# A selective-scan stage on one core: two 512-column scans per step become one of 1024 columns

## The chip, the core and the metric

The program runs on one core of one Trainium2 chip. The metric is the device time of one execution in microseconds (us). Engines: TensorE (PE), VectorE (DVE), ScalarE (ACT), GpSimd (POOL), and SyncE (SP), which here only issues DMAs.

## The reference

The program has two layers. The change lies in the first half of layer 1, a Mamba-like block over 4096 tokens in four sequences of 1024, with 512 channels and 16 states per channel. In short (x, z, B, C and dt come from projections of the normalised input):

```python
x     = silu(conv4(in_proj(h)))
dt    = softplus(wd2(wd1(x)) + bias)
decay = exp(dt * A)                 # per token, channel, state; A = -exp(A_log)
h[t]  = decay[t] * h[t-1] + dt[t] * x[t] * B[t]
y[t]  = sum over states (h[t] * C[t]) + W_D * x[t]
out   = out_w(y * silu(skip))
```

The recurrence starts from zero at the beginning of each sequence. Layer 0 (a gated recurrent block and an MLP) comes before it, a mixture of eight experts after it.

## The kernel before

Function `mamba` holds channels on the 128 partitions (so 512 channels are KE = 4 tiles) and tokens on the free axis. Tokens are cut into NCH = 8 chunks of T = 512; chunks 2k and 2k+1 are the two halves of sequence k. A chunk q has NU = 32 steps n, one for each state (NST = 16) and each pair of channel tiles (HALF = 2); u = 32q + n counts the steps. Of step u:

- POOL (`inputs`, L1103): `bx[u % 5] = ux * B`, 128x1024, that is two tiles of 512 columns. It works up to NB = 5 steps ahead, bound by `s_scan`.
- ACT (`decay`, L1251): two exponentials of 512 columns, one for each tile, into one of NA = 4 PSUM tiles `da`. The tile is free when the scan that used it two steps earlier is done.
- DVE (L1387): two scans of 512 columns, `hh = da * previous + bx`. In even chunks they start from 0.0, in odd chunks from `carry`, the last column of the same state in the chunk before, which ACT saved (`keep`, L1260).
- PE (`spread`, L1460): C[t] to all partitions, into the single PSUM tile `cb`.
- DVE (L1395): `hc = hh * cb`, 128x1024.
- PE (L1486): adds `hc` into `y` by a product with the identity.

After steps 16 and 32 of a chunk DVE forms `y * silu(skip)` (`finish`, L1373).

The order of the work is written out by hand, and each engine takes its own instructions in that order. Besides the steps, each engine has work for other chunks at fixed step numbers (`extra` on ACT and POOL, `pieces` on PE). Those that matter here:

- ACT, n = 0 to 11: convolution taps of chunk q+1 (`taps`, L1150, L1152), skip tiles (`take_skip`, L1159), n = 10 and 12: two output tiles of chunk q-1 (`take_out`, L1197), n = 12: `silu` (a table load, L1164, L1165, a table load back at the next exponential), n = 25: the exponential and logarithm of the softplus (L1226, a table load, L1229).
- POOL, n = 1, 4, 7, 10: sums of the taps (`conv`, L1032, L1034), which wait for ACT's taps; n = 26: L1083, which waits for ACT's L1229; n = 24 to 31: further softplus work (L1077, L1088, L1050) and, every five steps, an indirect DMA (L1112).
- PE: a projection piece on even n. One PSUM tile `rb` serves them all, so a piece waits until ACT has copied the one before.

ACT runs two steps ahead with its exponentials. Its loop is:

```python
for u in range(STEPS):
    if u + 2 < STEPS:
        decay(u + 2, 0)
    keep(u)
    if u + 2 < STEPS:
        decay(u + 2, 1)
    extra(u // NU, u % NU)
```

Of the kernel before, what the change touches and what calls it, by code (L numbers as in the profile page):

```python
# [6 lines left out]
P = 128  # L7
F32 = mybir.dt.float32
# [4 lines left out]
ALU = mybir.AluOpType  # L13
ACT = mybir.ActivationFunctionType
# [6 lines left out]
T = 512  # L21
NCH = NTOK // T
# [712 lines left out]
NST = 16  # L735
# [13 lines left out]
def mamba(nc, dram):  # L749
# [5 lines left out]
    HALF = KE // 2  # L755
    NB = 5
    NA = 4
    NG = 4
    NU = 2 * NST
# [16 lines left out]
    turn = {key: k for k, key in enumerate(order)}  # L776
# [3 lines left out]
    with ExitStack() as ctx:  # L780
        def sb(name, shape, dt=F32):
            return ctx.enter_context(nc.sbuf_tensor("m_" + name, shape, dt))

        def sem(name):
            return ctx.enter_context(nc.semaphore("m_" + name))

        y = ctx.enter_context(nc.psum_tensor("m_y", [P, HALF, T], F32))
        da = [ctx.enter_context(nc.psum_tensor(f"m_da{i}", [P, T], F32)) for i in range(NA)]
        cb = ctx.enter_context(nc.psum_tensor("m_cb", [P, T], F32))
        rb = ctx.enter_context(nc.psum_tensor("m_rb", [P, T], F32))  # L790
        dram["held"] = ExitStack()
# [11 lines left out]
        A = sb("A", [P, KE * NST])  # L803
# [12 lines left out]
        dl = [sb(f"dl{h}", [P, KE, T]) for h in range(2)]  # L816
# [9 lines left out]
        bx, hc = work[:, 0:NB], work[:, NB:NB + 4]  # L826
        rows = sb("rows", [P, 2, REC])
        hh = sb("hh", [P, 2, HALF, T])
        mo = sb("mo", [P, 2, D])
        mo2 = hh[:, 0, 0].rearrange("p (s d) -> p s d", d=D)  # L830
        dst = sb("dst", [P, NPICK], I32)
        carry = sb("carry", [P, NST, KE])

        plan = hc.rearrange("p a b t -> p (a b t)")
        used = [0]

        def part(shape, dt=F32):
# [6 lines left out]
            if dt is not F32:  # L844
# [21 lines left out]
        filled, drained = sem("filled"), sem("drained")  # L866
# [4 lines left out]
                                                         sem("s_hc"), sem("s_y"))  # L871
        s_y1, s_diag, s_hi, s_res, s_mid, s_low = (sem("s_y1"), sem("s_diag"), sem("s_hi"), sem("s_res"), sem("s_mid"),
                                                   sem("s_low"))
        block = ctx.enter_context(nc.Block())

        def wait_filled(eng, g, p):
# [131 lines left out]
        def _(pool):  # L1008
# [83 lines left out]
            def inputs(u):  # L1092
                q, n = u // NU, u % NU
                if n % NST == 0:
                    pool.wait_ge(s_ux, 2 * q + n // NST + 1)
                if n % NG == 0:
                    G = u // NG
                    pool.wait_ge(b_in[G % 2], 16 * (G // 2 + 1))
                if u >= NB:
                    pool.wait_ge(s_scan, (u - NB + 1) * HALF)  # L1100
                cols = slice(HALF * (n // NST), HALF * (n // NST + 1))
                slot = bb[:, (u // NG) % 2, n % NG:n % NG + 1]
                pool.tensor_tensor(bx[:, u % NB], ux[q % 2][:, cols], slot.to_broadcast([P, HALF, T]), ALU.mult).then_inc(s_bx, 1)  # L1103
# [26 lines left out]
        def _(act):  # L1130
# [109 lines left out]

            def decay(u, i):
                q, n = u // NU, u % NU
                if n % NST == 0 and i == 0:
                    act.wait_ge(s_dl, 2 * q + n // NST + 1)
                    act.wait_ge(s_A, 1)
                d = u * HALF + i
                if d >= NA:
                    act.wait_ge(s_scan, d - NA + 1)
                e = HALF * (n // NST) + i
                at = e * NST + n % NST  # L1250
                act.activation(da[d % NA][:], dl[q % 2][:, e], ACT.Exp, scale=A[:, at:at + 1]).then_inc(s_exp, 1)  # L1251

            def keep(u):
                q, n = u // NU, u % NU
                if q % 2 == 0:
                    act.wait_ge(s_scan, (u + 1) * HALF)
                    if q >= 2:
                        act.wait_ge(s_scan, (u - NU + 1) * HALF)
                    j = n // NST
                    act.activation(carry[:, n % NST, HALF * j:HALF * (j + 1)], hh[:, u % 2, :, T - 1], ACT.Copy).then_inc(s_carry, 1)  # L1260

            act.wait_ge(s_pad, 1)
            for q, n in slots[:8 + NU]:
                if (q, n) == (-1, 27):
                    extra(q, n)
                    for u in range(2):
                        decay(u, 0)
                        decay(u, 1)
                    continue
                extra(q, n)  # L1270
                if (q, n) == (-2, 28):
                    act.wait_ge(s_d, 2 * NJ + 1)
                    act.activation(ex[:, 1], ex[:, 0], ACT.Exp).then_inc(s_ex, 1)
# [6 lines left out]
                extra(u // NU, u % NU)  # L1280
            take_out(NCH - 1, 0)
            wait_filled(act, "O1", NCH - 1)
            act.activation(mo2, da[0][:].rearrange("p (s d) -> p s d", s=2), ACT.Copy).then_inc(drained, 1)

        @block.vector
        def _(dve):
# [9 lines left out]
            def over(row, k):  # L1296

                return row.rearrange("p (o n) -> p o n", o=1).to_broadcast([row.shape[0], k, row.shape[1]])

            dve.wait_ge(lg_in, 16)  # L1300
            for j in range(NJ):
                step(dve.max(m8[:, j], lg[:, j]), False)
# [72 lines left out]
            for u in range(STEPS):  # L1375
                q, n = u // NU, u % NU
                j = n // NST
                dve.wait_ge(s_bx, u + 1)
                if u >= 2:
                    dve.wait_ge(s_hc, u - 1)  # L1380
                if u >= 2 and ((u - 2) // NU) % 2 == 0:
                    dve.wait_ge(s_carry, (u - 2) // NU // 2 * NU + (u - 2) % NU + 1)
                for i in range(HALF):
                    d = u * HALF + i
                    e = HALF * j + i
                    dve.wait_ge(s_exp, d + 1)
                    dve.tensor_tensor_scan(hh[:, u % 2, i], da[d % NA][:], bx[:, u % NB, i],  # L1387
                                           0.0 if q % 2 == 0 else carry[:, n % NST, e:e + 1], ALU.mult, ALU.add).then_inc(s_scan, 1)
                dve.wait_ge(s_cb, u + 1)
                dve.wait_ge(s_scan, (u + 1) * HALF)  # L1390
                if u >= 4:
                    dve.wait_ge(s_y, u - 3)
                else:
                    dve.wait_ge(s_out, 32)
                dve.tensor_tensor(hc[:, u % 4], hh[:, u % 2],  # L1395
                                  cb[:].rearrange("p (o t) -> p o t", o=1).to_broadcast([P, HALF, T]), ALU.mult).then_inc(s_hc, 1)
                if n == 0 and q > 0:
                    finish(q - 1, 1)
                if n == NST:
                    finish(q, 0)  # L1400
# [3 lines left out]
        def _(pe):  # L1404
# [5 lines left out]
            pe.wait_ge(s_diag, KE)  # L1410

            def piece(g, p):
                to = da[0] if (g, p) == ("O1", NCH - 1) else rb
                if turn[g, p] > 0 and to is rb:
                    pe.wait_ge(drained, turn[g, p])
                if g[:2] in ("IN", "SK"):
                    e = int(g[2:])
                    if g == "IN0":
                        pe.wait_ge(xr_in, p * 16 + 16)
                    col = (E_IN if g[:2] == "IN" else 0) + e * P  # L1420
                    for k in range(KD):
                        last = mm(rb[:], w_si[:, k, col:col + P], xr[:, k], start=(k == 0), stop=(k == KD - 1))
                elif g == "BD":
                    if p == 0:
                        pe.wait_ge(w_in, 16 * len(w_loads))
                    pe.wait_ge(s_silu, 2 * p + 1)
                    for e in range(KE):
                        last = mm(rb[0:DR + 2 * NST, :], w_x[:, e], xs[p % 2][:, e], start=(e == 0), stop=(e == KE - 1))
                elif g[:2] == "DT":
                    e = int(g[2:])  # L1430
                    wait_drained(pe, "BD", p)
                    last = mm(rb[:], w_dt[:, e * P:(e + 1) * P], dr, start=True, stop=True)
                else:
                    j = int(g[1:])
                    pe.wait_ge(s_y1, 2 * p + 2)
                    pe.wait_ge(res_in, 16 * (p + 1))
                    for s in (2 * j, 2 * j + 1):
                        at = slice((s % 2) * D, (s % 2 + 1) * D)
                        mm(to[:, at], ident[:], xres[:, s], start=(s % 2 == 0), stop=False, skip_group_check=True)
                        for e in range(KE):  # L1440
                            last = mm(to[:, at], y1[e // HALF][p % 2][:, e % HALF, s * P:(s + 1) * P], w_out[:, e],
                                      start=False, stop=(e == KE - 1 and s % 2 == 1), skip_group_check=True)
                last.then_inc(filled, 1)
# [28 lines left out]
            for u in range(STEPS):  # L1472
                q, n = u // NU, u % NU
                j = n // NST
# [441 lines left out]
```

## Time and profile before

| | us |
|---|---|
| median of three executions | 2537.9 (2536.19 to 2542.38) |
| profiled execution, its own span | 2537.0 |
| first scan of the step loop starts | 819.0 |
| last scan of the step loop starts | 1806.9 |
| PE, DVE, ACT, POOL busy over the span | 2135.7, 1956.4, 1376.4, 1328.8 |

The profile's span covers the first to the last instruction, and the profiled execution agrees with the median within 1 us. "Busy" is time in which an engine executed; the share over the whole span mixes the stages, so the step loop is read by itself. In a row of the timeline the numbers are the start, the time to the end of the group, engine, line, operation, written and read tensors; "x2" says that two instructions stand in one row, and a bracket gives the idle time before it and who ended it.

### The profile page before, as it was taken

What the parts mean: (1) busy time and instruction counts of PE and PEld (TensorE: products, weight loads), DVE (VectorE), ACT (ScalarE), POOL (GpSimd) and SP (SyncE); (2) the same over time, 40 slices, a digit from 0 to 9 for tenths busy, and PEclk for the clock granted to TensorE, in tenths of its full rate; (3) what the DMA queues carried; (4) which work ended last, traced back from release to release, by engine and by line L of the source; (5) the groups of instructions that cost most, each with busy time, mean ns of one, the idle gap of its engine ahead of it and who ended that gap; (6) DMA issues with size and microseconds to landing.
All of it is one profiled execution on the core that took longest, in us unless ns stands there. A gap on an engine that the chain in (4) does not pass through costs nothing. (4 is left out here: it accounts for less than half of the span.)

```text
span 2537.0 us, 35012 instructions
## 1 busy us (share of the span) xinstructions
PE 2135.7 (84%) x10706; PEld 1539.2 (61%) x10706; DVE 1956.4 (77%) x2684; ACT 1376.4 (54%) x2333; POOL 1328.8 (52%) x953
## 2 busy tenths in 40 slices
PE   2699999999975788788878887867599999999995
PEld 1578777787751334333334333323399999999995
DVE  6644565545645999989898999899688888888883
ACT  1322233222326676667666666653277777777672
POOL 1112221122206999898989899997213333334433
PEclk8899999999987999999999999999899999999998
DMA  8010111101122213232223232314166667667663
GB/s 267 17 42 0 41 41 41 41 0 41 41 68 89 105 69 109 75 105 77 100 77 103 75 105 75 115 57 165 59 240 227 206 228 235 208 222 236 212 216 88
DMA packets 108971, 286.66 MB, mean 113 GB/s; under 512 B 20550, under 2 KB 85462, under 8 KB 90022
## 3 DMA queue, kind: packets, MB, share of 16 engines
q1 hardware_dynamic: 94598, 267.12, 30.1%
q0 software_dynamic: 14304, 18.75, 3.6%
q8 instruction: 27, 0.44, 0.1%
q14 instruction: 42, 0.34, 0.0%
HBM read 239.21 MB, written 50.82 MB: 114 GB/s over the span
## 5 line engine op out<-in xcount | busy, mean ns | idle before, releaser
L1103 POOL TENSOR_TENSOR m_work<-m_ux,m_bb 128x1024 f32<-128x1024 f32 x256 | 598.5, 2358 | 24.7 <-DVE m_hh L1387 22.1
L1251 ACT ACTIVATE m_da<-m_dl,m_A 128x512 f32<-128x512 f32 x512 | 349.3, 687 | 279.6 <-DVE m_hh L1387 278.8
L1486 PE MATMUL m_y<-m_work,m_ident 128*128 128x512 f32 x1024 | 493.0, 604 | 1.5 <-DVE m_work L1395 1.5
L1806 PE MATMUL e_h<-e_xTh,e_w1h 128*128 128x256 f32 x1248 | 353.4, 283 | 7.2 <-DVE e_xTl L1742 6.5
L1395 DVE TENSOR_TENSOR m_work<-m_hh,m_cb 128x1024 f32<-128x1024 f32 x256 | 312.7, 1222 | 48.8 <-PE m_cb L1460 25.6
L1806 PE MATMUL e_h<-e_xTl,e_w1h 128*128 128x256 f32 x1248 | 349.4, 280 | 0.0
L1806 PE MATMUL e_h<-e_xTh,e_w1l 128*128 128x256 f32 x1248 | 349.3, 280 | 0.0
L1387 DVE TENSOR_TENSOR_SCAN m_hh<-m_da,m_carry,m_work 128x512 f32<-128x512 f32 x256 | 313.9, 1268 | 7.4 <-POOL m_work L1103 7.3
L1387 DVE TENSOR_TENSOR_SCAN m_hh<-m_da,m_work 128x512 f32<-128x512 f32 x256 | 298.3, 1208 | 13.4 <-POOL m_work L1103 13.4
L1486 PEld LDWEIGHTS m_y<-m_work,m_ident 128*128 128x128 f32 x1024 | 198.3, 194 | 161.0 <-issue 147.9
L281 POOL TENSOR_TENSOR small<-mv,eps_ln 128x4 f32<-128x4 f32 x17 | 3.4, 201 | 551.3 <-DVE mv L399 551.3
L1460 PE MATMUL m_cb<-m_bc,m_sel 96*128 96x512 bf16 x256 | 98.3, 384 | 192.5 <-DVE m_work L1395 192.1
L1702 ACT ACTIVATE e_sg<-e_h,e_b 128x256 f32<-128x256 f32 x312 | 146.4, 470 | 187.1 <-PE e_h L1806 187.1
L1806 PEld LDWEIGHTS e_h<-e_xTh,e_w1h 128*128 128x128 f32 x1248 | 237.4, 190 | 8.0 <-DVE e_xTl L1742 5.3
L1460 PEld LDWEIGHTS m_cb<-m_bc,m_sel 96*128 96x128 bf16 x256 | 24.7, 96 | 356.8 <-DVE m_work L1395 343.0
L1806 PEld LDWEIGHTS e_h<-e_xTl,e_w1h 128*128 128x128 f32 x1248 | 235.6, 189 | 0.0
L1806 PEld LDWEIGHTS e_h<-e_xTh,e_w1l 128*128 128x128 f32 x1248 | 235.3, 189 | 0.0
L1759 DVE SCALAR_TENSOR_TENSOR e_ac<-e_h,e_b,e_sg 128x256 f32<-128x256 f32 x312 | 149.4, 479 | 44.6 <-ACT e_sg L1702 44.1
L1817 PE MATMUL e_o<-e_w2h,e_ach 128*128 128x256 f32 x624 | 174.1, 279 | 0.0
L1587 POOL DMA_INDIRECT scratch_mo<-e_yo,e_place x78 | 160.8, 2062 | 24.4 <-issue 11.9
L1817 PE MATMUL e_o<-e_w2h,e_acl 128*128 128x256 f32 x624 | 173.3, 278 | 0.0
L1817 PE MATMUL e_o<-e_w2l,e_ach 128*128 128x256 f32 x624 | 173.1, 277 | 0.0
(275 smaller groups left out, 4801.0 us busy)
## 6 DMA issues: line engine op xcount, KB each, us to landing
m_bb<-scratch_bT SPq DMA_DIRECT2D x64, 1024.0 KB
m_first<-in_w SPq DMA_DIRECT2D x20, 2048.0 KB, 7.5
e_w<-in_w SPq DMA_DIRECT2D x19, 2048.0 KB, 7.4
m_first<-in_w SPq DMA_DIRECT2D x20, 1024.0 KB, 10.1
e_w<-in_w SPq DMA_DIRECT2D x19, 1024.0 KB, 10.0
scratch_rec<-x1p SPq DMA_DIRECT2D x39, 260.0 KB, 8.3
e_xg<-scratch_rec SPq DMA_DIRECT2D x39, 260.0 KB, 2.8
e_b<-in_b SPq DMA_DIRECT2D x39, 128.0 KB, 3.0
```

What stands on the lines that cost most here:

```text
L281: pool.tensor_tensor(sm[:, 0], var, eps_ln[:], ALU.add).then_inc(done, 1)
L1103: pool.tensor_tensor(bx[:, u % NB], ux[q % 2][:, cols], slot.to_broadcast([P, HALF, T]), ALU.mult).then_inc(s_bx, 1)
L1251: act.activation(da[d % NA][:], dl[q % 2][:, e], ACT.Exp, scale=A[:, at:at + 1]).then_inc(s_exp, 1)
L1387: dve.tensor_tensor_scan(hh[:, u % 2, i], da[d % NA][:], bx[:, u % NB, i], 0.0 if q % 2 == 0 else carry[:, n % NST, e:e + 1], ALU.mult, AL ...
L1395: dve.tensor_tensor(hc[:, u % 4], hh[:, u % 2], cb[:].rearrange("p (o t) -> p o t", o=1).to_broadcast([P, HALF, T]), ALU.mult).then_inc(s_ ...
L1460: mm(cb[:], sel[:, at:at + 1].to_broadcast([3 * 2 * NST, P]), bc3[q % 2][:], start=True, stop=True).then_inc(s_cb, 1)
L1486: last = mm(y[:, i], ident[:], hc[:, u % 4, i], start=False, stop=(n % NST == NST - 1))
L1587: pool.indirect_dma_start(dram["mo"][:, :], bass.IndirectOffsetOnAxis(ap=place[i][:, s:s + 1], axis=0), yo[i][:, s, :], None, compute_op=A ...
L1702: act.activation(sg[:, m % 2], hbank[m % HR][:, 1], ACT.Silu, bias=b1[i][:, KF + m:KF + m + 1]).then_inc(s_sg, 1)
L1759: dve.scalar_tensor_tensor(out=ac[:, m % 2], in0=hbank[m % HR][:, 0], scalar=b1[i][:, m:m + 1], in1=sg[:, m % 2], op0=ALU.add, op1=ALU.mul ...
L1806: last = mm(hbank[m % HR][:, j], w[i][:, k, cols], x[i][:, k], start=(p == 0 and k == 0 and j == 0), stop=(p == 2 and k == KD - 1 and j == 1),
L1817: last = mm(obank[i][:, s], a[i][:, m, s * P:(s + 1) * P], w[i][:, m], start=(m + s + p == 0), stop=(p == 2 and m == KF - 1 and s == NS - ...
```

## The change

The four `da` tiles become one PSUM tensor of 4 x 512 columns, so that the pair of a step is 1024 adjacent columns. DVE makes one scan over both tiles of a step. So that the second tile doesn't continue from the end of the first, its first decay column is zero: it is written once, at the start, and the exponential of tile 1 writes columns 1 to 511 only. In odd chunks tile 1 has a carry of its own; ACT adds `a0 * carry` to the first column of its `bx` (one 128x1 instruction per step, `a0` being 16 first decays, computed in one 128x16 exponential for each half of an odd chunk). This new instruction stands on ACT ahead of the exponential of tile 1 and waits for POOL's `bx` of its step. Both exponentials of a step now wait for the one scan two steps earlier.

```diff
-        da = [ctx.enter_context(nc.psum_tensor(f"m_da{i}", [P, T], F32)) for i in range(NA)]
+        da = ctx.enter_context(nc.psum_tensor("m_da", [P, NA, T], F32))
...
+        a0 = sb("a0", [P, HALF, NST])
...
                 if u >= NB:
-                    pool.wait_ge(s_scan, (u - NB + 1) * HALF)
+                    pool.wait_ge(s_scan, u - NB + 1)
...
             def decay(u, i):
                 q, n = u // NU, u % NU
+                j = n // NST
+                e = HALF * j + i
                 if n % NST == 0 and i == 0:
-                    act.wait_ge(s_dl, 2 * q + n // NST + 1)
+                    act.wait_ge(s_dl, 2 * q + j + 1)
                     act.wait_ge(s_A, 1)
+                    if q % 2 == 1:
+                        act.activation(a0[:, j], A[:, (e + 1) * NST:(e + 2) * NST], ACT.Exp,
+                                       scale=dl[q % 2][:, e + 1, 0:1]).then_inc(s_a0, 1)
                 d = u * HALF + i
-                if d >= NA:
-                    act.wait_ge(s_scan, d - NA + 1)
-                e = HALF * (n // NST) + i
+                if u >= 2:
+                    act.wait_ge(s_scan, u - 1)
+                if q % 2 == 1 and i == 1:
+                    act.wait_ge(s_bx, u + 1)
+                    act.wait_ge(s_a0, q // 2 * 2 + j + 1)
+                    act.wait_ge(s_carry, q // 2 * NU + n + 1)
+                    head = bx[:, u % NB, 1, 0:1]
+                    act.activation(head, carry[:, n % NST, e:e + 1], ACT.Identity, scale=a0[:, j, n % NST:n % NST + 1],
+                                   bias=head).then_inc(s_fix, 1)
                 at = e * NST + n % NST
-                act.activation(da[d % NA][:], dl[q % 2][:, e], ACT.Exp, scale=A[:, at:at + 1]).then_inc(s_exp, 1)
+                act.activation(da[:, d % NA, i:T], dl[q % 2][:, e, i:T], ACT.Exp, scale=A[:, at:at + 1]).then_inc(s_exp, 1)
...
-                for i in range(HALF):
-                    d = u * HALF + i
-                    e = HALF * j + i
-                    dve.wait_ge(s_exp, d + 1)
-                    dve.tensor_tensor_scan(hh[:, u % 2, i], da[d % NA][:], bx[:, u % NB, i],
-                                           0.0 if q % 2 == 0 else carry[:, n % NST, e:e + 1], ALU.mult, ALU.add).then_inc(s_scan, 1)
+                dve.wait_ge(s_exp, (u + 1) * HALF)
+                if u == 0:
+                    dve.wait_ge(s_cut, HALF)
+                if q % 2 == 1:
+                    dve.wait_ge(s_fix, q // 2 * NU + n + 1)
+                pair = slice(u % 2 * HALF, u % 2 * HALF + HALF)
+                e = HALF * j
+                dve.tensor_tensor_scan(hh[:, u % 2].rearrange("p e t -> p (e t)"), da[:, pair].rearrange("p e t -> p (e t)"),
+                                       bx[:, u % NB].rearrange("p e t -> p (e t)"),
+                                       0.0 if q % 2 == 0 else carry[:, n % NST, e:e + 1], ALU.mult, ALU.add).then_inc(s_scan, 1)
```

ACT's instructions around step 12 of an odd chunk, before; L1251 is an exponential of `decay`, L1197 `take_out`, L1164 and L1165 `silu`:

```order
L1197 ACTIVATE m_mo<-m_rb 128x512 [waits m_filled]
L1251 ACTIVATE m_da<-m_dl,m_A 128x512 [waits m_s_scan] x4
L1197 ACTIVATE m_mo<-m_rb 128x512 [waits m_mo_out,m_filled]
L1164 ACT_TABLE_LOAD [waits m_drained]
L1164 ACTIVATE m_xs<-m_spare 128x2048 [waits m_s_cv]
L1165 ACTIVATE m_sk<-m_sk 128x2048
L1251 ACT_TABLE_LOAD
L1251 ACTIVATE m_da<-m_dl,m_A 128x512 [waits m_s_scan] x2
```

The same place of the changed program (lines have moved: L1264 is the exponential, L1261 the new 128x1 instruction, L1199 `take_out`, L1166 and L1167 `silu`):

```order
L1199 ACTIVATE m_mo<-m_rb 128x512 [waits m_filled]
L1264 ACTIVATE m_da<-m_dl,m_A 128x512 [waits m_s_scan]
L1261 ACTIVATE m_work<-m_carry,m_work,m_a 128x1 [waits m_s_a0,m_s_carry,m_s_bx,m_s_scan]
L1264 ACTIVATE m_da<-m_dl,m_A 128x511
L1264 ACTIVATE m_da<-m_dl,m_A 128x512 [waits m_s_scan]
L1261 ACTIVATE m_work<-m_carry,m_work,m_a 128x1 [waits m_s_a0,m_s_carry,m_s_bx,m_s_scan]
L1264 ACTIVATE m_da<-m_dl,m_A 128x511
L1199 ACTIVATE m_mo<-m_rb 128x512 [waits m_mo_out,m_filled]
L1166 ACT_TABLE_LOAD [waits m_drained]
L1166 ACTIVATE m_xs<-m_spare 128x2048 [waits m_s_cv]
L1167 ACTIVATE m_sk<-m_sk 128x2048
L1264 ACT_TABLE_LOAD
```

What moved: between any two extras of an odd chunk there now stands an instruction that waits for `s_bx`, POOL's product.

DVE around step 0 of an odd chunk, before:

```order
L1387 SCALAR_TENSOR_TENSOR m_hh<-m_da,m_carry,m_work 128x512 [waits m_s_carry,m_s_exp,m_s_hc,m_s_bx]
L1387 SCALAR_TENSOR_TENSOR m_hh<-m_da,m_carry,m_work 128x512 [waits m_s_exp]
L1395 TENSOR_TENSOR m_work<-m_hh,m_cb 128x1024 [waits m_s_y,m_s_scan,m_s_cb]
L1373 TENSOR_TENSOR m_y<-m_y,m_sk 128x1024 [waits m_s_silu,m_s_y]
L1387 SCALAR_TENSOR_TENSOR m_hh<-m_da,m_carry,m_work 128x512 [waits m_s_carry,m_s_exp,m_s_hc,m_s_bx]
```

And after, the scan (L1406) of two steps:

```order
L1406 SCALAR_TENSOR_TENSOR m_hh<-m_da,m_carry,m_work 128x1024 [waits m_s_exp,m_s_carry,m_s_fix,m_s_hc,m_s_bx]
```

What moved: one instruction of 1024 columns stands where two of 512 stood, and it waits for both exponentials and for the new instruction (`s_fix`).

## Rows read from the trace of the kernel before

**Rows 1.** The page, part 1: busy us (share of the span) xinstructions.

```profile
PE 2135.7 (84%) x10706; PEld 1539.2 (61%) x10706; DVE 1956.4 (77%) x2684; ACT 1376.4 (54%) x2333; POOL 1328.8 (52%) x953
```

**Rows 2.** Stretches, chunks 1 and 7: length, busy of PE, PEld, DVE, ACT, POOL, PE clock.

```profile
937.00:1062.30 125.30, 102.36 (x258) 44.56 (x256) 117.66 (x100) 82.82 (x116) 117.33 (x57) 0.97 0.26 90
...
1687.90:1811.00 123.10, 83.53 (x212) 36.50 (x212) 117.19 (x99) 42.70 (x62) 84.25 (x40) 0.97 0.27 98
```

**Rows 3.** Waits in the step loop: engine line waited for, us in total, times, longest.

```profile
DVE m_work L1395 <- PE m_cb L1460: 25.6, 18, 2.7
...
POOL m_spare L1083 <- ACT m_spare L1229: 21.1, 7, 3.7
DVE m_hh L1387 <- POOL m_work L1103: 20.7, 14, 4.5
```

**Rows 4.** Tile view of m_work: durations min/median/max in ns, first and last start, form.

```profile
L1387 DVE TENSOR_TENSOR_SCAN m_hh<-m_da,m_work x256: 1196/1207/1225, 819.0 to 1685.4; 128x512 f32<-128x512 f32 x128
...
L1387 DVE TENSOR_TENSOR_SCAN m_hh<-m_da,m_carry,m_work x256: 1257/1267/1284, 937.0 to 1806.9; 128x512 f32<-128x512 f32 x128
...
L1331 DVE TENSOR_TENSOR_SCAN m_work<-m_work x8: 260/270/2382, 760.9 to 764.4; 128x64 f32<-128x64 f32 x8
```

**Rows 5.** Timeline, DVE: a step of chunk 3, then one of chunk 4.

```profile
1291.85 2.45 DVE L1387 TENSOR_TENSOR_SCAN m_hh<-m_da,m_carry,m_work 128x512 f32<-128x512 f32 x2
1294.39 1.22 DVE L1395 TENSOR_TENSOR m_work<-m_hh,m_cb 128x1024 f32<-128x1024 f32 x1
...
1318.98 2.33 DVE L1387 TENSOR_TENSOR_SCAN m_hh<-m_da,m_work 128x512 f32<-128x512 f32 x2
...
1321.40 1.22 DVE L1395 TENSOR_TENSOR m_work<-m_hh,m_cb 128x1024 f32<-128x1024 f32 x1
```

**Rows 6.** Groups by line and form, ACT: count, busy us, mean ns, idle before.

```profile
L1150 ACT ACTIVATE m_spare<-m_first,m_vec 128x512 f32<-128x512 f32 x84 | 57.0, 711 | 31.7 <-issue 31.7
...
L1260 ACT ACTIVATE m_carry<-m_hh 128x2 f32<-128x2 f32 x128 | 26.0, 203 | 37.8 <-DVE m_hh L1387 37.6
...
L1152 ACT ACTIVATE m_spare<-m_first,m_vec 128x512 f32<-128x512 f32 x28 | 22.5, 803 | 0.0
```

**Rows 7.** Timeline of chunk 1, steps 10 to 15: POOL, then ACT, then DVE.

```profile
992.09 4.69 POOL L1103 TENSOR_TENSOR m_work<-m_ux,m_bb 128x1024 f32<-128x1024 f32 x2
...
989.45 0.58 ACT L1197 ACTIVATE m_mo<-m_rb 128x512 f32<-128x512 f32 x1
990.05 1.28 ACT L1164 ACT_TABLE_LOAD   x1
992.16 1.91 ACT L1164 ACTIVATE m_xs<-m_spare 128x2048 f32<-128x2048 f32 x1 [0.83 <-POOL m_spare L1034]
993.98 1.90 ACT L1165 ACTIVATE m_sk<-m_sk 128x2048 f32<-128x2048 f32 x1
995.89 1.28 ACT L1251 ACT_TABLE_LOAD   x1
997.19 3.15 ACT L1251 ACTIVATE m_da<-m_dl,m_A 128x512 f32<-128x512 f32 x5
...
998.17 1.28 DVE L1387 TENSOR_TENSOR_SCAN m_hh<-m_da,m_carry,m_work 128x512 f32<-128x512 f32 x1
```

**Rows 8.** Timeline: POOL's product and DVE's scan, chunk 3, then chunk 5.

```profile
1240.88 2.36 POOL L1103 TENSOR_TENSOR m_work<-m_ux,m_bb 128x1024 f32<-128x1024 f32 x1
...
1249.85 1.28 DVE L1387 TENSOR_TENSOR_SCAN m_hh<-m_da,m_carry,m_work 128x512 f32<-128x512 f32 x1
...
1492.44 4.67 POOL L1103 TENSOR_TENSOR m_work<-m_ux,m_bb 128x1024 f32<-128x1024 f32 x2
...
1499.62 1.28 DVE L1387 TENSOR_TENSOR_SCAN m_hh<-m_da,m_carry,m_work 128x512 f32<-128x512 f32 x1
```

**Rows 9.** Timeline of chunk 1, step 25: ACT, then POOL.

```profile
1039.61 1.04 ACT L1226 ACTIVATE m_spare<-m_spare 128x1024 f32<-128x1024 f32 x1
...
1044.02 2.35 POOL L1083 TENSOR_TENSOR m_spare<-m_spare 128x1024 f32<-128x1024 f32 x1 [2.45 <-ACT m_spare L1229]
```

More of the change, by code:

```diff
@@ L873, in mamba @@
                                                    sem("s_low"))
+        s_cut, s_a0, s_fix = sem("s_cut"), sem("s_a0"), sem("s_fix")
         block = ctx.enter_context(nc.Block())
@@ L1255, in keep @@
                 if q % 2 == 0:
-                    act.wait_ge(s_scan, (u + 1) * HALF)
+                    act.wait_ge(s_scan, u + 1)
                     if q >= 2:
-                        act.wait_ge(s_scan, (u - NU + 1) * HALF)
+                        act.wait_ge(s_scan, u - NU + 1)
                     j = n // NST
@@ L1262, in _ @@
             act.wait_ge(s_pad, 1)
+            act.wait_ge(s_cut, HALF)
             for q, n in slots[:8 + NU]:
@@ L1282, in _ @@
             wait_filled(act, "O1", NCH - 1)
-            act.activation(mo2, da[0][:].rearrange("p (s d) -> p s d", s=2), ACT.Copy).then_inc(drained, 1)
+            act.activation(mo2, da[:, 0].rearrange("p (s d) -> p s d", s=2), ACT.Copy).then_inc(drained, 1)
         @block.vector
@@ L1298, in over @@
                 return row.rearrange("p (o n) -> p o n", o=1).to_broadcast([row.shape[0], k, row.shape[1]])
+            for i in range(HALF):
+                dve.memset(da[:, 2 * i + 1, 0:1], 0.0).then_inc(s_cut, 1)
             dve.wait_ge(lg_in, 16)
@@ L1382, in _ @@
                     dve.wait_ge(s_carry, (u - 2) // NU // 2 * NU + (u - 2) % NU + 1)
-                for i in range(HALF):
-                    d = u * HALF + i
-                    e = HALF * j + i
-                    dve.wait_ge(s_exp, d + 1)
-                    dve.tensor_tensor_scan(hh[:, u % 2, i], da[d % NA][:], bx[:, u % NB, i],
-                                           0.0 if q % 2 == 0 else carry[:, n % NST, e:e + 1], ALU.mult, ALU.add).then_inc(s_scan, 1)
+                dve.wait_ge(s_exp, (u + 1) * HALF)
[8 more added lines that the diff above has]
+                                       0.0 if q % 2 == 0 else carry[:, n % NST, e:e + 1], ALU.mult, ALU.add).then_inc(s_scan, 1)
                 dve.wait_ge(s_cb, u + 1)
-                dve.wait_ge(s_scan, (u + 1) * HALF)
+                dve.wait_ge(s_scan, u + 1)
                 if u >= 4:
@@ L1412, in piece @@
             def piece(g, p):
-                to = da[0] if (g, p) == ("O1", NCH - 1) else rb
-                if turn[g, p] > 0 and to is rb:
+                own = (g, p) == ("O1", NCH - 1)
+                to = da[:, 0] if own else rb[:]
+                if turn[g, p] > 0 and not own:
                     pe.wait_ge(drained, turn[g, p])
```

## The prediction

> **What bounds the kernel now.** I read the page first [rows 1]: over the span PE is the busiest engine, but that is a mean over stages, and the change touches only the step loop. So I cut the loop into its eight chunks. In chunk 1 DVE is busy 117.66 and POOL 117.33 of 125.30 us; in chunk 7, where POOL has no work for a next chunk, POOL needs only 84.25 while DVE needs 117.19 of 123.10 [rows 2]. Two engines are nearly full, so the waits decide. DVE waits 20.7 us for POOL's products and 25.6 us for the spread C; POOL in turn waits 21.1 us, 3 us in each of seven chunks, for ACT's logarithm [rows 3]. The chain of a chunk is therefore a ring, not one engine: ACT's work of step 25, which begins with L1226 at 1039.61 and goes through a table load and L1229, releases POOL's L1083 at 1044.02 after 2.45 us of idleness [rows 9]; POOL then runs without a pause through its softplus and convolution work up to the steps near 14 of the next chunk, where DVE has caught up with it; from there DVE goes at its own pace to step 25. A faster scan helps on the last arc alone. Chunk 7 is DVE's from its third step on, chunk 0 in all its steps.
>
> **What a scan of 1024 columns saves.** A 64-column scan takes 270 ns and a 512-column one 1207: (1207 - 270) / 448 = 2.09 ns a column, 136 ns fixed. So 1024 columns are 2.28 us, and 60 ns more with a carry (1267 against 1207) [rows 4]. Two scans of 512 take 2.33 us together without and 2.45 with a carry, since the second begins before the first has ended; the product L1395 follows 0.09 us later in both [rows 5]. The saving is 2.33 - 2.28 = 0.05 us a step in even chunks and 2.45 - 2.34 = 0.11 in odd ones: 128 x 0.16 = 20.5 us if every step counted. The Trainium skill (VectorE: DVE Perf Modes, the section on the fixed extra latency per instruction) says that the latency is exposed between instructions and a large tile pays it once; with its fixed term of about 150 cycles, 156 ns, the saving would be 256 x 0.156 = 40 us. The trace shows most of the fixed time already overlapped.
>
> **What the change costs on ACT, even chunks.** Both exponentials of step u+2 now wait for the whole scan of step u. Before, the first ran during the second scan of the pair. So everything behind them on ACT comes one exponential later, 0.62 us (five take 3.15, the last 0.69: (3.15 - 0.69) / 4) [rows 7]. The step's own exponentials have slack: their scan comes a product, a scan and a product later, 1.22 + 2.3 + 1.22 = 4.7 us [rows 5]. What is late is the logarithm of step 25, and with it POOL's L1083 and the ring: +0.6 a chunk. Against it stand the DVE steps of the last arc, from about 17 to 25, 8 x 0.05 = 0.4. An even chunk comes out at +0.2; chunks 2, 4, 6: **+0.6**. Chunk 0 has 25 steps at DVE's pace, 1.25 - 0.6, with a little lost at the silu: **-0.5**.
>
> **The new instruction, odd chunks.** No 128x1 instruction with two per-partition operands is in the trace. A 128x2 copy takes 203 ns; a second such operand costs 803 - 711 = 92 ns [rows 6]. Bounds: 203 ns, and 203 + 2 x 92 = 387. I take 0.38, of which 0.1 overlaps the next: 0.28 on ACT's chain. The Trainium skill (ScalarE: Activation LUTs, what an ACTIVATE costs) gives 93 ns for each pointer operand, as the trace has it. The 32 steps of a chunk have 9 us of this on an engine that is idle a third of the time [rows 2], so the work itself is hidden.
>
> What isn't hidden is what it waits for. It waits for `bx` of step u+2 at ACT's step u, and `extra(u)` stands behind it. To cost nothing, `bx` would have to be ready when the exponential of tile 0 ends, 4.7 - 0.7 = 4 us before its scan. It isn't: the product of step 14 ends at 994.45, 1243.24 and 1494.8 in chunks 1, 3 and 5 [rows 7, 8], and the scan of step 14 starts one step of 3.68 (2.54 + 1.22, less the 0.08 by which a scan starts before the product ends) ahead of that of step 15: leads of 0.0, 2.9 and 1.1 us. So ACT's extras now follow POOL instead of DVE, and whoever waits for them is late: PE's pieces (rb is drained later), through them `cb`, and most of all the silu. In chunk 1 `bx` of step 14 is ready at 992.09 + half of 4.69, 994.45. Behind it on ACT: new instruction 0.28, exponential 0.62, take_out 0.60, table load 1.30, silu 1.82 and 1.91, table load 1.30 (starts 989.45, 990.05, 992.16, 993.98, 995.89, 997.19), exponential 0.62, new instruction 0.28, exponential 0.69, and 0.03 of signal: 9.45 us. The scan of step 15 can't start before 1003.9; before it started at 998.17 [rows 7]. That is +5.7. For chunk 3, 1243.24 + 9.45 against 1249.85: +2.8. For chunk 5, 1494.8 + 9.45 against 1499.62: +4.6 [rows 8]. DVE gets back 10 x 0.11 = 1.1 until the scan of step 25; the logarithm then comes 0.62 + 0.28 = 0.9 later behind it. Net -0.2 each: 5.5 + 2.6 + 4.4 = **+12.5**. POOL's own chain up to step 14 I leave as it is: the taps end about when the convolution asks for them.
>
> Chunk 7 has neither taps nor silu: 28 x 0.11 = **-3.1**.
>
> The rest costs nothing: two memsets at the start, two 128x16 exponentials for an odd chunk (about as long as the 203 ns copy, in idle ACT time), one scan semaphore in place of two.
>
> **Sum.** 12.5 + 0.6 - 0.5 - 3.1 = +9.5 us. The sum is made on the profiled execution (2537.0), 0.9 below the median; I put it on the median: 2547.4, and as POOL's chain can only suffer by late taps, **2548**.
>
> **Rivals.** *DVE sets the pace* (the other side). If POOL kept far enough ahead at steps 0 to 14 of the odd chunks, no wait of the new instruction would be seen, and the scan's saving would count in full: -20.5 us, 2517; half of it, 2528, if the ring keeps half. For it: DVE is at 94% in a chunk. Against it: 20.7 us of waiting for POOL, and a POOL as full as DVE. It decides from a lead of about 4 us. With the page's 156 ns it would be 2498. Chance 0.13.
>
> *The new wait is absorbed.* The silu's lateness finds slack that I don't see (DVE waits 25.6 us for PE, some of it just behind, at steps 10 to 12 and 16 [rows 3]). Then odd chunks lose 1 us or nothing: -3.1 - 0.5 + 0.6 + 3 = 0, so 2532 to 2541. Chance 0.27.
>
> *It goes round twice.* ACT's taps, too, stand behind `bx`, and POOL's convolution asks for them. From the `bx` of the step ahead of a tap pair ACT needs 0.28 + 0.62, two taps 1.2, 0.62 + 0.28 + 0.62 of the next step, and taps 0.62 + 0.80 plus a skip tile 0.6 at times: 5.0 to 5.6 us; POOL asks after two products, 4.7. At 0.3 to 0.9 us for each of four convolutions in three chunks that is 12 x 0.6 = 7 us on POOL's own arc, on top of my sum: 2555. Chance 0.15.
>
> My forecast, the silu behind `bx`, 2541 to 2553: 0.45.
>
> **Numbers.** A measurement of this kernel can tell about 0.3%, 7.6 us: faster is below 2530.3, slower above 2545.5. Faster 0.13 (first rival). Slower: 0.15 of the last rival and three quarters of my own, 0.34: 0.49. Same: 0.38. The range that leaves out 0.1 at either end is 2531 to 2559.
>
> **What the profile after would show.** Right: a scan of 1024 columns at 2.28 and 2.34 us; in odd chunks ACT's 128x1 instruction with idle time released by POOL's product; in chunks 1, 3, 5 a gap of several us before the scan of step 15, released by an exponential; POOL's L1083 later by the same; chunk 7 shorter by 3 us, odd chunks longer by 3 to 5.5, even ones unchanged. Wrong: if odd chunks have no gap before step 15, POOL was ahead and the silu was not the neck; if a 1024-column scan takes much more than 2.28 us, the linear price fell; if the even chunks change by over 1 us, the ring is read wrongly.

## The result and the profile after

The changed kernel takes 2553.82 us (median, 2553.12 to 2554.74), the kernel before 2538.26 in the same comparison: ratio 1.0059, 95% interval 1.0045 to 1.0073. It is slower by 15.6 us. 2548 was forecast, in a range of 2531 to 2559; the band that I gave to this cause alone, 2541 to 2553, is passed by 0.8 us.

The step loop, from the start of the first scan to the end of the last product L1395 (L1415 in the changed kernel), takes 1002.6 us in the profiled execution after and 990.5 before: +12.1. The whole span grew from 2537.0 to 2551.6. Of the 2.4 us that this leaves, 0.47 lie ahead of the loop and 1.95 behind it, in code that the change doesn't touch. That part behind it takes 727.5 us before, 729.5 after, and 728.1 to 729.6 in the twelve runs below; the profiled execution of before was a short one there. I therefore compare loops beside medians. A loop is that of one execution, though, and not only the edit moves it: chunks 0 and 4 of wait_at_14 below, in which nothing was edited, came out 1.2 and 1.1 us longer than before.

The groups of DVE's product and of its scans, from the profile page of the changed kernel (out<-in, count, busy us, mean ns, idle before):

```profile
L1415 DVE TENSOR_TENSOR m_work<-m_hh,m_cb 128x1024 f32<-128x1024 f32 x256 | 312.6, 1221 | 62.5 <-PE m_cb L1481 41.3
...
L1406 DVE TENSOR_TENSOR_SCAN m_hh<-m_da,m_carry,m_work 128x1024 f32<-128x1024 f32 x128 | 300.1, 2344 | 21.2 <-ACT m_da L1264 20.8
L1406 DVE TENSOR_TENSOR_SCAN m_hh<-m_da,m_work 128x1024 f32<-128x1024 f32 x128 | 292.3, 2283 | 18.3 <-POOL m_work L1105 16.5
```

The scan of 1024 columns takes 2.28 us and 2.34 with a carry, as the straight line through [rows 4] gave. DVE has less work, but before it never waited for ACT's exponentials and now it waits 20.8 us for them, and its wait for the spread C has grown from 25.6 [rows 3] to 41.3 us.

Stretches of the changed kernel, chunks 0 to 3 and 7 (columns as in [rows 2], where the last two are the share of the DMA engines and GB/s):

```profile
819.50:936.20 116.70, 88.70 (x208) 35.01 (x209) 110.82 (x66) 82.58 (x146) 108.02 (x53) 0.99 0.24 87
936.20:1068.90 132.70, 106.78 (x260) 45.80 (x259) 114.41 (x67) 90.47 (x151) 118.19 (x58) 0.95 0.24 85
1068.90:1192.60 123.70, 101.31 (x254) 44.20 (x254) 112.24 (x67) 83.26 (x149) 114.07 (x57) 0.97 0.27 93
1192.60:1324.80 132.20, 106.68 (x260) 45.68 (x259) 114.32 (x68) 90.44 (x151) 118.09 (x58) 0.95 0.24 85
...
1701.90:1824.00 122.10, 86.49 (x212) 37.52 (x212) 113.83 (x66) 49.83 (x95) 84.75 (x40) 0.94 0.27 99
```

Chunk 1 has gone from 125.3 to 132.7 us, its DVE work from 117.66 to 114.41. By the starts of their first scans the eight chunks changed by -1.3, **+7.4**, -0.6, **+4.5**, -0.1, **+4.6**, -1.1 and -1.3 us: the loss sits in chunks 1, 3 and 5 alone.

The place that was forecast, step 12 of chunk 1, timeline of ACT, then DVE, changed kernel:

```profile
994.75 0.39 ACT L1261 ACTIVATE m_work<-m_carry,m_work,m_a 128x1 f32<-128x1 f32 x1 [2.30 <-POOL m_work L1105]
995.04 0.67 ACT L1264 ACTIVATE m_da<-m_dl,m_A 128x511 f32<-128x511 f32 x1
995.65 0.57 ACT L1199 ACTIVATE m_mo<-m_rb 128x512 f32<-128x512 f32 x1
996.24 1.28 ACT L1166 ACT_TABLE_LOAD   x1
997.54 1.92 ACT L1166 ACTIVATE m_xs<-m_spare 128x2048 f32<-128x2048 f32 x1
999.36 1.89 ACT L1167 ACTIVATE m_sk<-m_sk 128x2048 f32<-128x2048 f32 x1
1001.27 1.28 ACT L1264 ACT_TABLE_LOAD   x1
1002.56 0.69 ACT L1264 ACTIVATE m_da<-m_dl,m_A 128x512 f32<-128x512 f32 x1
1003.19 0.37 ACT L1261 ACTIVATE m_work<-m_carry,m_work,m_a 128x1 f32<-128x1 f32 x1
1003.47 0.67 ACT L1264 ACTIVATE m_da<-m_dl,m_A 128x511 f32<-128x511 f32 x1
...
998.04 2.34 DVE L1406 TENSOR_TENSOR_SCAN m_hh<-m_da,m_carry,m_work 128x1024 f32<-128x1024 f32 x1
1000.47 1.22 DVE L1415 TENSOR_TENSOR m_work<-m_hh,m_cb 128x1024 f32<-128x1024 f32 x1
1004.34 2.35 DVE L1406 TENSOR_TENSOR_SCAN m_hh<-m_da,m_carry,m_work 128x1024 f32<-128x1024 f32 x1 [2.64 <-ACT m_da L1264]
```

ACT stands idle for 2.30 us until POOL's product, then the chain of [rows 7] follows link by link, and the scan of step 15 starts at 1004.34 instead of 998.17. Counted from the first scan of its chunk it comes 7.0, 4.2 and 6.1 us later in chunks 1, 3 and 5; that of step 14 comes 4.4, 2.2 and 4.1 us later. So a good part of the lateness is there ahead of the silu. The new instruction takes 0.37 to 0.39 us.

A second hole, at steps 4 to 6 of the same chunk; timeline of ACT, PE and DVE:

```profile
962.39 0.39 ACT L1261 ACTIVATE m_work<-m_carry,m_work,m_a 128x1 f32<-128x1 f32 x1 [1.82 <-issue]
...
964.61 0.57 ACT L1161 ACTIVATE m_sk<-m_rb 128x512 f32<-128x512 f32 x1
...
965.24 3.78 PE L1443 MATMUL m_rb<-m_xr,m_first 128*128 128x512 f32 x4 [6.02 <-ACT m_sk L1161]
968.81 0.64 PE L1481 MATMUL m_cb<-m_bc,m_sel 96*128 96x512 bf16 x1
...
969.49 1.22 DVE L1415 TENSOR_TENSOR m_work<-m_hh,m_cb 128x1024 f32<-128x1024 f32 x1 [3.58 <-PE m_cb L1481]
```

The skip tile (L1161) is copied late, since it too stands behind a wait for `bx`: the profile names no releaser for the 1.82 us ahead of L1261, but its start is 0.1 us behind the end of a product of POOL, 962.3. PE can't start its piece in `rb`, and DVE waits 3.58 us for the spread C behind the piece. The product that waits is that of step 6; the scan of step 7 comes late by it, hence "the hole at step 7" below. Chunks 3 and 5 have the same hole, with 3.48 and 3.40 us. I had named this path, but not priced it.

### The profile page after: what moved, and what is told of

The parts are those of the page before. It is cut to its first block and busy times, and to the rows that moved or that the text cites. A ratio compares the mean times of both kernels' runs of the same rounds, so it can differ in the third digit from the quotient of the medians.

```text
span 2551.6 us, 35270 instructions
## 1 busy us (share of the span) xinstructions
PE 2151.4 (84%) x10706; PEld 1543.8 (61%) x10706; DVE 1937.8 (76%) x2430; ACT 1396.6 (55%) x2469; POOL 1330.8 (52%) x953
## 5 line engine op out<-in xcount | busy, mean ns | idle before, releaser
L1264 ACT ACTIVATE m_da<-m_dl,m_A 128x512 f32<-128x512 f32 (+1 forms) x512 | 346.3, 679 | 245.3 <-DVE m_hh L1406 245.0
L1415 DVE TENSOR_TENSOR m_work<-m_hh,m_cb 128x1024 f32<-128x1024 f32 x256 | 312.6, 1221 | 62.5 <-PE m_cb L1481 41.3
L1406 DVE TENSOR_TENSOR_SCAN m_hh<-m_da,m_carry,m_work 128x1024 f32<-128x1024 f32 x128 | 300.1, 2344 | 21.2 <-ACT m_da L1264 20.8
L1406 DVE TENSOR_TENSOR_SCAN m_hh<-m_da,m_work 128x1024 f32<-128x1024 f32 x128 | 292.3, 2283 | 18.3 <-POOL m_work L1105 16.5
L1443 PE MATMUL m_rb<-m_xr,m_first 128*128 128x512 f32 x256 | 137.5, 663 | 63.0 <-ACT m_sk L1161 28.2
```

Of the source, the lines that this page charges most:

```text
L1264: act.activation(da[:, d % NA, i:T], dl[q % 2][:, e, i:T], ACT.Exp, scale=A[:, at:at + 1]).then_inc(s_exp, 1)
L1406: dve.tensor_tensor_scan(hh[:, u % 2].rearrange("p e t -> p (e t)"), da[:, pair].rearrange("p e t -> p (e t)"), bx[:, u % NB].rearrange("p ...
L1415: dve.tensor_tensor(hc[:, u % 4], hh[:, u % 2], cb[:].rearrange("p (o t) -> p o t", o=1).to_broadcast([P, HALF, T]), ALU.mult).then_inc(s_ ...
```

## The experiments

Twelve kernels ran. Theory A, mine: in odd chunks ACT's extras are held up behind the wait for POOL's product. Theory B: both exponentials waiting for one scan delay the ring. Theory C: the added instructions load ACT. All medians beside runs of the kernel before on the same chip; loops from the profiled executions (before: 990.5).

```
label                    median us (before)   ratio, 95% interval        loop us
the change               2553.8 (2538.3)      1.0059 (1.0045, 1.0073)    1002.6
wait_only                2548.4 (2539.3)      1.0031 (1.0015, 1.0046)    1002.0
joint_wait               2545.4 (2539.3)      1.0021 (1.0009, 1.0034)     996.2
no_bx_wait               2535.9 (2539.3)      0.9983 (0.9972, 0.9994)     984.6
fix_one_step_later       2544.1 (2539.3)      1.0014 (0.9999, 1.0029)     994.2
late_only_14             2552.5 (2538.7)      1.0057 (1.0043, 1.0070)    1005.2
late_up_to_12            2546.2 (2538.7)      1.0025 (1.0014, 1.0035)     997.2
wait_at_14               2554.1 (2539.5)      1.0061 (1.0048, 1.0074)    1002.9
wait_not_at_14           2548.6 (2539.5)      1.0040 (1.0027, 1.0053)     998.6
even_chunks_only         2545.7 (2539.5)      1.0033 (1.0020, 1.0046)     994.8
log_before_decay         2523.4 (2539.5)      0.9937 (0.9923, 0.9950)     974.3
change_and_log_first     2535.1 (2538.6)      0.9986 (0.9974, 0.9998)     984.1
late_12_and_log_first    2533.7 (2538.6)      0.9980 (0.9971, 0.9989)     984.9
```

**The wait alone, added to the kernel before.**

```diff
                 if d >= NA:
                     act.wait_ge(s_scan, d - NA + 1)
+                if q % 2 == 1 and i == 1:
+                    act.wait_ge(s_bx, u + 1)
```

> The kernel before with one line more: in odd chunks ACT waits for POOL's product of its step ahead of the exponential of tile 1. No merged scan, no new instruction. Theory A (ACT's extras are held up behind that wait; the silu of step 12 is the neck): 12 to 16 us slower than before, a gap ahead of the scan of step 15 in chunks 1, 3 and 5. Theory B (the loss is that both exponentials wait for the whole scan two steps earlier, which delays the logarithm of step 25) and theory C (the added instructions load ACT): within 3 us of before.

Median +9.1, loop +11.5. No instruction is added, and by the medians 9.1 of the change's 15.6 us are there. C falls as the main cause. The median is below the 12 to 16 that I expected, and of the three gaps ahead of the scan of step 15 only one is there, 1.3 us in chunk 1: DVE has already lost 3.3, 1.7 and 3.4 us by step 14, waiting for the spread C. The profiled execution was the slowest of the eleven, 8.0 us above their median, so its loop overstates this kernel.

**The joint wait alone**, in the kernel before: `act.wait_ge(s_scan, (u - 1) * HALF)` for both exponentials.

> The kernel before, but both exponentials of a step wait for the second scan of the step two earlier, in all chunks. Theory B: 10 us slower or more. Theory A: only the logarithm and with it the ring of each chunk comes 0.6 us later, 3 to 6 us slower than before. Theory C: no change.

Median +6.1, loop +5.7, at the upper end of what A has. That is 0.8 for each of seven chunks on average (0.6 was my price), but single chunks lie between -1.2 and +1.9, so one execution doesn't confirm a price per chunk. It is a real cost of the change, but not the largest.

**The change without its wait.** The new instruction writes into a scratch column and waits for no product; so this kernel leaves out the carry of tile 1.

```diff
-                    act.wait_ge(s_bx, u + 1)
...
-                    head = bx[:, u % NB, 1, 0:1]
-                    act.activation(head, carry[:, n % NST, e:e + 1], ...
+                    act.activation(aside[:, u % 2:u % 2 + 1], carry[:, n % NST, e:e + 1], ...
```

> The changed kernel, but the 128x1 instruction writes aside and doesn't wait for POOL's product; so tile 1 of each pair starts an odd chunk without its carry. Everything else of the change stays, the instruction too. Theory A: 3 to 8 us faster than before (scan saving without the gap), 2530 to 2536. Theories B and C: within 3 us of the changed kernel, 2551 or more.

2535.9, 3.4 below before; loop -5.9. So the merged scan does pay a little when the wait is gone, even with the joint wait still in, and the wait costs 1002.6 - 984.6 = 18 us of loop. Here the scan of step 15 of chunk 1 waits only 0.82 us:

```profile
990.25 1.91 ACT L1167 ACTIVATE m_xs<-m_spare 128x2048 f32<-128x2048 f32 x1 [0.17 <-POOL m_spare L1037]
...
997.05 2.35 DVE L1405 TENSOR_TENSOR_SCAN m_hh<-m_da,m_carry,m_work 128x1024 f32<-128x1024 f32 x1 [0.82 <-ACT m_da L1263]
```

The silu starts at 990.25, not at 997.54.

**The new instruction one step later**, complete. It is taken out of `decay`, and the loop begins with it:

```diff
             for u in range(STEPS):
+                if u + 1 < STEPS and late(u + 1):
+                    fix(u + 1)
                 if u + 2 < STEPS:
                     decay(u + 2, 0)
```

`late` is true in all steps of odd chunks for the first of the next three, for step 14 alone in the second, up to step 12 in the third.

> The changed kernel, complete, but the 128x1 instruction of step u+1 stands at the head of ACT's step u, behind the extras of step u-1, in place of that of step u+2 in its middle. It needs POOL's product one step later. Theory A: most of the loss is gone, 2533 to 2542. Theories B and C: no change against the changed kernel, 2551 or more.

> The changed kernel, complete; only the 128x1 instruction of step 14 of odd chunks stands one step later, behind the silu of step 12. If the silu behind the product of step 14 is the neck (my step of the sum), the scan of step 15 comes as early as DVE's own lateness at step 14 allows: 2.7, 2.0 and 2.0 us earlier in chunks 1, 3 and 5 (from the trace of the changed kernel), 5 to 7 us faster than it. If the hole at step 7 (skip tiles late, so spread C late) is what counts, no change.

> The changed kernel, complete; the 128x1 instructions of steps 0 to 12 of odd chunks stand one step later, those of steps 13 to 31 as in the change. The hole at step 7 should close (the scan of step 8 comes 3 us earlier in odd chunks). If the silu is the neck, the scan of step 15 stays where it is and the time is within 2 us of the changed kernel. If the hole at step 7 is what counts: 8 to 12 us faster than it.

The first gains 10 us on the change and ends 2 us above the 2533 to 2542 that I expected. It isn't back at before, since the instruction now stands behind extras, where the scan waits for it: in chunk 1 3.24 us at step 2 (taps), 1.35 at step 14 (silu) and 1.06 at step 27 (logarithm). The other two contradicted me: moving step 14 alone gave 1.3 us in place of 5 to 7, which the intervals don't tell from nothing; moving steps 0 to 12 gave 7.6, where I expected 2 at most if the silu was the neck and 8 to 12 if the hole at step 7 was. The timeline of the second shows why it isn't a clean test; ACT and DVE of late_only_14:

```profile
997.21 0.37 ACT L1256 ACTIVATE m_work<-m_carry,m_work,m_a 128x1 f32<-128x1 f32 x1
...
997.71 2.35 DVE L1419 TENSOR_TENSOR_SCAN m_hh<-m_da,m_carry,m_work 128x1024 f32<-128x1024 f32 x1 [1.01 <-ACT m_work L1256]
...
1001.29 2.34 DVE L1419 TENSOR_TENSOR_SCAN m_hh<-m_da,m_carry,m_work 128x1024 f32<-128x1024 f32 x1
...
1009.00 1.22 DVE L1428 TENSOR_TENSOR m_work<-m_hh,m_cb 128x1024 f32<-128x1024 f32 x1 [1.79 <-PE m_cb L1494]
```

The scan of step 15 does come earlier, but not by the 3 us between 1001.29 and 1004.34: chunk 1 began 1.5 us earlier in this execution. Counted from the chunk's first scan it is 1.6 us in chunk 1, and 0.7 and 1.0 in chunks 3 and 5 (2.7, 2.0 and 2.0 expected). The instruction of step 14 now waits behind the silu itself, and at step 16 DVE waits for PE instead. In late_up_to_12 the scan of step 15 stays late, as expected if the silu is the neck (6.6, 3.4 and 5.1 us within chunks 1, 3 and 5, against 7.0, 4.2 and 6.1 in the change), but its total isn't within 2 us of the change. So I asked the same with waits alone.

**The wait at one step, and at all others**, in the kernel before: the condition of wait_only with `and n == 14`, then with `and n != 14`.

> The kernel before with ACT's wait for POOL's product ahead of the exponential of tile 1 at one step only, step 14 of each odd chunk, which is the one ahead of the silu. Theory N (the silu behind the product of step 14 is the neck of odd chunks): the scan of step 15 comes 5.2, 2.2 and 4.0 us later in chunks 1, 3 and 5 (8.9 us behind the product, one 128x1 instruction less than in the change), 8 to 11 us slower than before. Theory S (the loss comes in at steps 4 to 8, by the skip tiles and the spread C): within 2 us of before.

> The kernel before with the same wait at all steps of odd chunks but step 14. Theory S alone: as wait_only, 9 to 11 us slower. Theory N alone: within 3 us of before. Both in parallel, each hiding the other: this run and the one with the wait at step 14 alone are each 5 to 10 us slower, and their sum exceeds wait_only.

One wait at four places of the program (step 14 of the odd chunks; chunk 7 has no silu and doesn't change) costs 12.4 us of loop, as much as all 128 of wait_only (11.5). Its median, +14.7, lies above the 8 to 11 that I expected. ACT and DVE of wait_at_14, chunk 1:

```profile
998.32 0.69 ACT L1253 ACTIVATE m_da<-m_dl,m_A 128x512 f32<-128x512 f32 x1 [6.18 <-POOL m_work L1103]
...
1006.68 2.46 DVE L1389 TENSOR_TENSOR_SCAN m_hh<-m_da,m_carry,m_work 128x512 f32<-128x512 f32 x2 [4.65 <-ACT m_da L1253]
```

The scan of step 15 comes 4.7, 1.8 and 3.6 us later within chunks 1, 3 and 5 (5.2, 2.2, 4.0 expected), while that of step 14 hasn't moved. Without that wait the others still cost 8.1; there the spread C is the one that holds DVE (wait_not_at_14):

```profile
966.02 2.46 DVE L1389 TENSOR_TENSOR_SCAN m_hh<-m_da,m_carry,m_work 128x512 f32<-128x512 f32 x2 [0.86 <-POOL m_work L1103]
972.90 1.22 DVE L1397 TENSOR_TENSOR m_work<-m_hh,m_cb 128x1024 f32<-128x1024 f32 x1 [4.42 <-PE m_cb L1462]
```

12.4 and 8.1 alone, 11.5 together: they lie in parallel. In chunks 1, 3 and 5 alone, without what the other chunks add by chance, it is 10.3, 8.1 and 10.1. DVE's lateness from step 7 on makes it arrive later at step 15, where the silu would have stopped it anyway: with all waits the scan of step 15 is 4.7, 1.9 and 3.6 us late, as with the wait at step 14 alone. The medians say the same more strongly: +14.7 and +9.1 alone, +9.1 together.

**The merged scan in even chunks alone**, with two scans and separate semaphores in odd ones.

> The change in even chunks alone: merged scan there, two scans of 512 and the old waits in odd chunks, no 128x1 instruction. Theory A (the wait for POOL's product costs the time): within 4 us of before, 2535 to 2541, since even chunks gained 0.1 to 1.3 us each in the trace of the changed kernel. If the merged scan itself or the joint wait cost it: 2543 or more.

A miss: 2545.7, which by what I wrote down would speak for the other side. But the even chunks came out shorter, by 2.6, 2.9, 0.7 and 1.6 us, and the odd ones longer, by 2.6, 2.4, 4.1 and 3.2, chunk 7 too, which should be untouched. DVE waits 23.7 us for its own second scan (114 times), which it doesn't before. In chunk 7 the product L1415 starts 0.20 us behind the end of the second scan, against 0.09 in [rows 5]: 0.11 us a step, some 3.5 a chunk. So my form of the odd chunks, with its two semaphores, costs about what the odd chunks lost; the run is no test of theory A, and nothing in it speaks against the merged scan in even chunks.

**The ring.** In the kernel before, step 25 alone:

```diff
+                if u % NU == 25:
+                    extra(u // NU, u % NU)
                 if u + 2 < STEPS:
                     decay(u + 2, 0)
                 keep(u)
                 if u + 2 < STEPS:
                     decay(u + 2, 1)
-                extra(u // NU, u % NU)
+                if u % NU != 25:
+                    extra(u // NU, u % NU)
```

> The kernel before; only at step 25 ACT does its extras (exponential and logarithm of the softplus) ahead of the exponentials of step 27 instead of behind them. If the ring through ACT's logarithm and POOL's L1083 sets the length of chunks 0 to 6, they come about 2 us earlier in each of seven chunks, and the exponentials of step 27 about 0.5 us too late: 7 to 14 us faster than before. If DVE's own work sets the pace: no gain, or a loss of 3 us.

2523.4, ratio 0.9937: 16 us faster than before, 2 more than the most that I expected. ACT's L1226 now follows the instruction ahead of it (L1191) at once; before, two exponentials and 1.1 us of waiting for DVE's scans stood between them, 2.4 us in all (1037.18 to 1039.61). In chunk 1 POOL no longer idles ahead of L1083, against 2.45 us in [rows 9]; over the loop that wait has gone from 21.1 to 4.7 us:

```profile
1036.90 0.68 ACT L1191 ACTIVATE m_spare<-m_rb,m_vec 128x512 f32<-128x512 f32 x1
1037.61 1.06 ACT L1226 ACTIVATE m_spare<-m_spare 128x1024 f32<-128x1024 f32 x1
...
1042.03 2.35 POOL L1083 TENSOR_TENSOR m_spare<-m_spare 128x1024 f32<-128x1024 f32 x1
```

Chunks 1 to 6 are 2.0 to 4.3 us shorter; chunk 7, which the prediction gave to DVE alone, is as long as before. That shows the ring which the prediction rests on. It is the fastest kernel here.

> The changed kernel, complete, with the extras of step 25 ahead of the exponentials of step 27. By the ring the logarithm comes 2 to 3 us earlier in each of chunks 0 to 6 (2.2 as before, and 0.6 to 0.9 that the joint wait and the 128x1 instruction cost there): 14 to 20 us faster than the changed kernel, 2534 to 2540, and still 10 us or more behind the kernel before with the same move. If the change's loss hung on the logarithm alone, both would come out equal, 2523.

> The changed kernel, complete, with the 128x1 instructions of steps 0 to 12 one step later and the extras of step 25 first. The two moves should add: 7 us from the first, 14 to 20 from the second, 2527 to 2533. To make the merged scan worth having it would have to be below 2523.

With the change the same move gives 18.8 us, more than without it (16). That fits the joint wait's share coming back too, which no run separates; but the change still ends 11.7 us behind. The two moves together were to reach 2527 to 2533 and gave 2533.7: they don't add. Moving steps 0 to 12 as well gives 1.4 us by the median in place of 7.6, and the two loops (984.1 and 984.9) don't show even that.

## Why the prediction was right

**Scan.** 2.28 and 2.34 us priced and measured. As a saving at the end it is worth little: with the new wait removed, but with the joint wait (+5.7 by itself), the loop is 5.9 us shorter, of the 20.5 that all steps would give.

**Even chunks.** I had +0.2 each for 2, 4, 6 and -0.5 for chunk 0; measured -0.6, -0.1, -1.1 and -1.3. The scan's saving over the chunk and the later logarithm nearly cancel, as forecast, but chunks 0 and 6 changed by more than the 1 us that I had named as a sign of a ring read wrongly. A chunk that no edit touches moves by 1.2 us too, so these rows can't decide that; log_before_decay does, and shows the ring.

**New instruction.** 0.38 us by the rows; 0.373 measured (median of 128).

**Odd chunks, the silu behind `bx`.** This carried the forecast: +5.5, +2.6, +4.4 for chunks 1, 3, 5 against +7.4, +4.5, +4.6, so 12.5 against 16.5. The mechanism is shown by wait_at_14; the size was low by a quarter. The scan of step 15 is 7.0, 4.2 and 6.1 us late where the sum had 5.7, 2.8 and 4.6. The chain from the end of the product of step 14 to the scan of step 15 is 9.7 us in all three chunks, 9.45 in the sum. POOL's product of step 14 comes 1.0 to 1.3 us later, counted from the chunk's first scan. Of that, 0.3 to 0.9 arise behind POOL's product of step 0, where I had left POOL's arc untouched (in the changed kernel its convolutions wait seven times for taps, 0.17 to 0.57 us, 2.0 in all: the third rival, in small). And I let DVE get back 1.1 us until step 25; in chunks 1 and 3 a further wait for PE near step 19 takes 0.8 us of that back, and in chunk 1 the scan of step 25 is still 6.5 us late within the chunk, against 7.0 at step 15. POOL's L1083 is later by about the same (7.2, 4.8 and 5.4 us), as forecast.

**Chunk 7.** -3.1 forecast, -1.3 measured: the new instruction's wait costs DVE 1.5 us at steps 2 and 3, where POOL is 1.2 us ahead.

**The sum.** Loop +9.5 forecast, +12.1 measured. That it is no further off is partly luck: odd chunks and chunk 7 were 4.0 and 1.8 us worse than forecast, the four even ones together 3.2 better, which chance alone could do (1.2 us a chunk).

**Rivals.** "DVE sets the pace" falls with the chunk lengths. "The new wait is absorbed" falls with no_bx_wait: 18 us of loop hang on the wait. "It goes round twice" was right in a part that I took for a repeat and which is a parallel path: skip tile, PE's piece, spread C. It alone costs 8.1 us, beside the silu nothing more. What I had priced for that rival, 7 us on POOL's own arc, came to 2.

Open: why the medians of wait_only (+9.1) and wait_at_14 (+14.7) differ by more than their loops (+11.5 and +12.4); their profiled executions lie 8.0 and 0.5 us above the medians, so wait_only's loop is probably too long. Open too: why the same wait costs 9 us by the median when it is added to the kernel before, but some 18 when it is taken out of the changed kernel, where each wait has the new instruction and the joint wait beside it.

## What to carry to other kernels

Merging two instructions saved 0.05 to 0.11 us a step, since most of their fixed time was already overlapped; the correction that the merge needed put one wait for POOL into each step of a queue whose steps had waited for DVE alone. Price such a wait by what stands behind it in the queue (here a 6 us block of silu and table loads), not by the instruction that waits. And look for the ring: where two engines are 94% busy, moving one block of a third engine ahead of work that has slack gave 16 us, where the merged scan on a busy engine gave 3.4 at best, without its wait.

## What the runs showed of the hardware

After 6.02 us without work, PE ran its next piece (L1443, four matmuls) in 3.78 us; the piece ahead of it took 1.99, and the median of the 52 pieces of the changed loop is 1.90. Chunks 3 and 5 have the same: 3.78 us after 6.34 and after 6.50 us without work. In the loop of the kernel before none took over 2.2 us. The granted clock over that stretch was 0.50, the 1.2 GHz level, and 1.00 (2.4 GHz) 2.3 us behind it. Stretches of the changed kernel (columns as in [rows 2]):

```profile
965.20:969.00 3.80, 3.76 (x5) 1.51 (x6) 0.70 (x1) 2.07 (x4) 3.72 (x3) 0.50 0.84 310
971.30:973.20 1.90, 1.90 (x5) 0.57 (x4) 1.81 (x2) 1.90 (x4) 1.87 (x2) 1.00 0.20 70
```

So at these three places the late release of PE cost its lateness and another 1.9 us. I hadn't priced that.
